# Ternary quantisation of the feed-forward weights: from ScalarE and GpSimd to GpSimd alone, ahead of the rest of its group

## The chip, the cores and the metric

One core of a Trainium2 chip. The time is that of the device for one execution, in microseconds; a kernel's figure is the median of its runs. A profiled execution gives the trace; its span goes from the first to the last instruction of the program.

Engines: TensorE (PE), its weight loads (PEld), VectorE (DVE), ScalarE (ACT), GpSimd (POOL). SyncE (SP) issues nearly all DMAs, in order.

## The reference, cut to what matters

A decoder layer with a layer norm behind each of its three parts: attention with 4-bit quantised projections, a cross attention, and a feed-forward part whose weights are ternary. 4 sequences of 512 tokens, 512 channels, 32 heads of 16. Of the feed-forward part:

```python
def weight_quant(w):
    scale = jnp.clip(jnp.mean(jnp.abs(w)), EPS)
    q = jnp.clip(jnp.round(w / scale), -1.0, 1.0) * scale
    return w + jax.lax.stop_gradient(q - w)

def h_bitlinear(x, w):
    xq = act_quant(fwht(x))          # Hadamard rotation, 8 bits per token
    wq = weight_quant(w)
    return jnp.einsum('bsh,oh->bso', xq, wq)

gate = h_bitlinear(hidden_states, w_gate)      # 512 -> 2048
up = h_bitlinear(hidden_states, w_up)
return h_bitlinear(jax.nn.silu(gate) * up, w_down)
```

So each of the three weight matrices (2048 x 512) becomes -1, 0 or 1 times one scale: -1 below half the scale's negative, 1 above half the scale.

## The kernel before, in words

Three stages follow each other. The first (up to about 150 us) quantises the inputs and the projection weights, computes the cross attention's maps, and reads all feed-forward weights once for their mean magnitudes; at its end f_rec holds, for each matrix, one over the scale. The second is the attention loop (to about 689 us). The third does the output projection, the cross attention's product, and the feed-forward part.

**The attention loop** goes over 32 groups (`groups`): 4 sequences (b) by 8 groups (r) of 4 heads. n is the group's number, and each engine has its own function for a group: `pe_period`, `act_period`, `dve_period`, `pool_period`, `sp_period`. Each engine runs its own list in the order in which it is written, and they meet at semaphores alone. A group has 8 steps (u). In each step TensorE computes two score tiles for the group after (L978; VectorE takes their row maxima, L1134) and two transposed ones for this group (L996, into the two banks of st_bank; ScalarE takes their exponentials, L1083). Each of the two banks is written again only after its exponential. In four steps TensorE also multiplies probabilities with values (L1010).

At the start of a group VectorE splits the 16 maxima into three bfloat16 parts (nm, L1153 to L1162), TensorE turns them (L983), VectorE copies them out (nm_T, L1177), and SP stores them (L1267).

**Even groups** also make the queries and keys of a later pair of groups (`pe_qk`, `dve_y`): for each of the two, ScalarE takes the high part (`act_high`, L1090, at u=4 and 6), GpSimd the residual (L1219), ScalarE the middle part (`act_middle`, L1094, at u=5 and 7), GpSimd the low part (L1221); SP then writes them out in six stores (L1248). Residuals and low parts are `pool_parts`. **Odd groups** project the values of the next sequence (`pe_v`) and normalise a context tile on GpSimd (`pool_norm`, L695) once SP's spread of reciprocals (L683, L685) has landed. In groups with r=7 GpSimd also centres four tiles (L791), in those with r=1 it scales four (L797), from the second or third sequence on.

**The order on SP** in a group (`sp_period`): store nm_T; load the stacks for the group after next (L1258); in odd groups the spread; the store of an attention result (`sp_pv`, L1263); in odd groups the read of the sums (`sp_sums`, L668), behind a wait for the landing of the `sp_pv` stores; in even groups the six stores of the parts, behind waits for the low parts, and the reciprocals (L672); and last the load of a piece of feed-forward weights (`sp_ffn`, L1291).

**The feed-forward weights** pass through the loop in 24 pieces of 128 x 1024 (PIECES), one in each of the groups 0 to 23. A piece is loaded in the group before into one half of f_ring (two halves, which lie in woT), and only after the piece before last in the same half is done (f_done). In its group ScalarE, at u=3, multiplies by f_rec and adds the constant MAGIC, which rounds (`act_ffn`, L1295); GpSimd clips to MAGIC -1 and +1 (L1301) and takes MAGIC away into f_int_all (L1303). In GpSimd's list this stands behind the residuals (even) or the normalisation (odd).

Of the kernel before, what the change touches and what calls it, by code (L numbers as in the profile page):

```python
# [18 lines left out]
P = 128  # L19
# [28 lines left out]
def decoder_layer(nc, io):  # L48
    whole = ExitStack()
    with whole:  # L50
# [806 lines left out]
        with stage:  # L857
# [9 lines left out]
            rs_bc = sb("rs_bc", [P, S])  # L867
            woT = sb("woT", [P, KD, D])
            f_ring = woT[:].rearrange("p k d -> p (k d)").rearrange("p (i c) -> p i c", i=2)
            bo_row = sb("bo_row", [NC, D])  # L870
            bo_tmp = w_int["v"][0:NC].rearrange("p k c m -> p (k c m)").bitcast(F32).rearrange("p (i d) -> p i d", i=2)
            bo_bf = bias_parts["v"][0:NC].rearrange("p k m -> p (k m)")
            neg_max = sb("neg_max", [P, 2, 16])
# [235 lines left out]
            def act_period(act, g):  # L1109
                even = g.h == 0  # L1110
                for u in range(8):
                    g_T, w = steps_T(g, u)
                    if g_T:
                        act_exp(act, g_T, w)
                    if u == 0 and not g.second:
                        act_pv(act, g + -2)
                    if even and g.has(2):
                        if u in HIGH_AT:
                            act_high(act, g.tile(2), HIGH_AT.index(u))
                        if u in MIDDLE_AT:  # L1120
                            act_middle(act, g.tile(2), MIDDLE_AT.index(u))
                    if g.b > 1 and g.r == 3 and 1 <= u <= 4:
                        act_round(act, g.b - 2, u - 1)
                    if u == 3 and g.n < PIECES:
                        act_ffn(act, g.n)
                    if not even and u == V_AT + 1 and g.b < NB - 1:

                        if g.b and g.s == 0:
                            act.wait_ge(pv_mm, 2 * 2 * KD * g.b)
                        act_v(act, g.b + 1, g.s)  # L1130
# [51 lines left out]
            def dve_context(dve, g, u):  # L1182
# [21 lines left out]
                if g.b == NB - 1:  # L1204
                    if g.r == 1 and u == 4:
                        dve_rtb_row(dve, 0, misc)
                    if g.r == 3 and u == 7:
                        dve.wait_ge(v_mm, KD * NB)
                        dve_bias_o(dve, 0, 0, misc, bo_row[:], bo_tmp, bo_bf)
                    if g.r == 4 and 1 <= u < 6:  # L1210
                        dve_bias_o(dve, 0, u, misc, bo_row[:], bo_tmp, bo_bf)

            def pool_parts(pool, t):

# [7 lines left out]
                                       ALU.subtract).then_inc(low_ready, 1)  # L1222

            def pool_period(pool, g):
                if g.h == 0 and g.has(2):
                    pool_parts(pool, g.tile(2))
                if g.h == 1 and g.n >= 5:
                    pool_norm(pool, (g.n - 5) // 2, rs_bc[:])
                if g.n < PIECES:
                    pool_ffn(pool, g.n)  # L1230
                if g.b and g.r == 7:
                    for ct in range(KD):
                        pool_center(pool, g.b - 1, ct)
# [31 lines left out]
            def sp_period(sp, g):  # L1265
# [14 lines left out]
                if g.n + 1 < PIECES:  # L1280
                    sp_ffn(sp, g.n + 1)
                if g.n == PIECES:
                    need(sp, "f_done", 2 * PIECES)
                    load_wo(sp, woT[:], bo_row[:])
                if (g.b, g.r) == (NB - 1, 5):
                    sp.wait_ge(qk_mm, 2 * NM)
                    sp.dma_start(x1[:], x_rows[0]).then_inc(E("x_in"), 16)

            def sp_ffn(sp, c):
                need(sp, "f_done", 2 * (c - 1))  # L1290
                sp.dma_start(f_ring[:, c % 2, :], io["ffn"][c]).then_inc(f_in[c % 2], 16)  # L1291

            def act_ffn(act, c):
                act.wait_ge(f_in[c % 2], 16 * (PIECES // FBUF + c // 2 + 1))
                did(act.activation(f_ring[:, c % 2, :], f_ring[:, c % 2, :], ACT.Identity, bias=magic[:],  # L1295
                                   scale=f_rec[:, c // FPW:c // FPW + 1]), "f_round")

            def pool_ffn(pool, c):
                raw = f_ring[:, c % 2, :]
                need(pool, "f_round", c + 1)  # L1300
                did(pool.tensor_scalar(raw, raw, MAGIC - 1.0, MAGIC + 1.0, ALU.max, ALU.min), "f_done")  # L1301
                need(pool, "f_done", 2 * c + 1)
                did(pool.tensor_scalar(f_int_all[:, c, :], raw, -MAGIC, None, ALU.add), "f_done")  # L1303

            def groups(eng, period):

# [942 lines left out]
```

## Time and profile before

| | us |
|---|---|
| three runs | 1225.28 (median), 1222.91, 1225.84 |
| profiled execution, its time | 1230.77 |
| its span | 1229.0 |
| PE, DVE, ACT, POOL busy | 969.5, 860.4, 694.1, 373.8 |
| mean granted TensorE clock | 0.918 of full speed |

A row of the timeline gives start and duration in us, the engine, the line of the kernel, the operation, what it writes and reads, and in brackets the time for which the engine had stood idle before it and who released it. SPq rows are the issues of DMAs, not their transfers. A row of the windows gives the stretch, its length, and for PE, PEld, DVE, ACT and POOL the busy time with the number of instructions, then the granted TensorE clock (1.00 is 2.4 GHz), the DMA engines' busy share and GB/s. A row of a source line gives shortest, median and longest duration in ns, and first and last start in us. Spans on POOL are rough.

### The profile page before, as it was taken

Reading aid. Unit: us, or ns where it says so; the run is one execution under the profiler, and the core shown is the slowest. Engines: PE = TensorE matmul, PEld = TensorE weight load, DVE = VectorE, ACT = ScalarE, POOL = GpSimd, SP = SyncE. Lnnn points to the kernel's source line nnn. Section 1 sums busy time; section 2 is a strip of 40 time slices with the busy share of each in tenths; the row PEclk is TensorE's granted clock in tenths of the full one; section 3 lists DMA queues with packets and bytes.
Section 4 is the critical chain, followed back from the end, with each engine's and each line's share of the span. In section 5 each row is a group of like instructions: output and inputs, shape, how many; then the busy total and the mean of one; then the engine's idle time right before and its main releaser. Section 6 shows DMA issues by size and latency. Waiting matters only on the chain. (4 is left out here: it accounts for less than half of the span.)

```text
span 1229.0 us, 13431 instructions
## 1 busy us (share of the span) xinstructions
PE 969.5 (79%) x4128; PEld 366.9 (30%) x4128; DVE 860.4 (70%) x1624; ACT 694.1 (56%) x1106; POOL 373.8 (30%) x296
## 2 busy tenths in 40 slices
PE   1556478988999888988988578988897799779565
PEld 0222112222222222222222243334443444334222
DVE  6854468888888998999896548837764776475245
ACT  2775425777777767776767224436633663365255
POOL 1000135546566567565301243122003101310000
PEclk9878668999999998999999879989998999899877
DMA  9873154555555555555523321321052105102500
GB/s 333 279 281 132 46 165 138 156 168 179 169 179 174 173 156 173 162 173 157 156 64 109 117 77 26 68 44 69 3 129 42 69 18 125 29 1 51 119 1 35
DMA packets 90798, 145.80 MB, mean 119 GB/s; under 512 B 12356, under 2 KB 52164, under 8 KB 89095
## 3 DMA queue, kind: packets, MB, share of 16 engines
q1 hardware_dynamic: 87270, 132.36, 36.6%
q10 hardware_dynamic: 3456, 12.58, 2.9%
q8 instruction: 33, 0.54, 0.2%
q14 instruction: 39, 0.31, 0.1%
HBM read 85.54 MB, written 42.21 MB: 104 GB/s over the span
## 5 line engine op out<-in xcount | busy, mean ns | idle before, releaser
L1134 DVE TENSOR_REDUCE neg_max<-banks 128x1 f32<-128x512 f32 x512 | 332.1, 683 | 55.1 <-PE banks L978 52.4
L1083 ACT ACTIVATE probs<-banks 128x512 f32<-128x512 f32 x512 | 278.9, 598 | 120.4 <-PE banks L996 115.8
L996 PE MATMUL banks<-q_st,k_st 99*128 99x512 bf16 x512 | 196.8, 387 | 34.1 <-ACT probs L1083 27.7
L978 PE MATMUL banks<-k_st,q_st 96*128 96x512 bf16 x512 | 201.6, 398 | 4.3 <-DMA k_st<-qk_parts 2.3
L1010 PE MATMUL banks<-probs,v_st 128*32 128x512 f32 x1024 | 138.2, 612 | 8.9 <-ACT pv_z L1107 7.7
L1670 PE MATMUL banks<-q_T,f_int_all 128*128 128x512 bf16 x512 | 125.8, 387 | 19.5 <-DVE h_ring L1691 19.4
L1464 POOL TENSOR_TENSOR rstd<-vare,half 128x1 f32<-128x1 f32 x48 | 26.8, 558 | 358.2 <-DVE vare L1456 358.2
L1729 PE MATMUL banks<-hz,I_h 128*128 128x512 f32 x128 | 71.3, 698 | 35.3 <-DMA hz<-h_turned 32.9
L996 PEld LDWEIGHTS banks<-q_st,k_st 99*128 99x128 bf16 x512 | 49.8, 98 | 133.5 <-ACT probs L1083 72.5
L978 PEld LDWEIGHTS banks<-k_st,q_st 96*128 96x128 bf16 x512 | 50.9, 100 | 127.5 <-DVE neg_max L1134 64.8
L1301 POOL TENSOR_SCALAR woT<-woT 128x1024 f32<-128x1024 f32 x24 | 87.2, 3632 | 2.4 <-ACT woT L1295 0.4
L1680 DVE TENSOR_TENSOR h_ring<-banks,gate_row 128x512 f32<-128x512 f32 x64 | 44.1, 689 | 59.9 <-PE banks L1670 58.3
L1685 ACT ACTIVATE h_ring<-h_ring 128x512 f32<-128x512 f32 x64 | 40.3, 630 | 77.4 <-DVE h_ring L1680 77.4
L1670 PEld LDWEIGHTS banks<-q_T,f_int_all 128*128 128x128 bf16 x512 | 48.7, 99 | 100.6 <-DVE h_ring L1691 28.8
L1708 ACT COPY h_turned<-banks 128x512 f32<-128x512 f32 x64 | 37.1, 582 | 62.0 <-DMA hz<-h_turned 37.2
L1812 PE MATMUL banks<-f_int_all,ctx_q 128*128 128x512 bf16 x256 | 61.5, 388 | 9.1 <-ACT ctx_q L1796 9.1
L1448 PE MATMUL banks<-attn_T,x_T 128*128 128x512 f32 x128 | 60.8, 620 | 9.5 <-DVE x L1487 7.9
L1748 DVE TENSOR_TENSOR h_max<-h_abs,h_max 128x512 f32<-128x512 f32 x60 | 44.4, 741 | 34.1 <-ACT h_abs L1737 32.7
L1734 ACT COPY hz<-banks 128x1024 f32<-128x1024 f32 x32 | 32.4, 1013 | 62.6 <-PE banks L1729 62.6
L1303 POOL TENSOR_SCALAR f_int_all<-woT 128x1024 bf16<-128x1024 f32 x24 | 66.7, 2779 | 2.0
L1702 PE MATMUL banks<-h_ring,had 128*128 128x512 f32 x128 | 64.4, 596 | 2.3 <-ACT h_turned L1708 2.3
L695 POOL TENSOR_TENSOR ctx_q<-ctx_q,rs_bc 128x512 f32<-128x512 f32 x14 | 17.8, 1270 | 153.2 <-DMA ctx_q<-pv_rows 153.2
(260 smaller groups left out, 1506.7 us busy)
## 6 DMA issues: line engine op xcount, KB each, us to landing
hz<-h_turned SPq DMA_DIRECT2D x64, 256.0 KB
f_int_all<-in_ffn_dram ACTq DMA_DIRECT2D x24, 512.0 KB, 6.9
woT<-in_ffn_dram SPq DMA_DIRECT2D x24, 512.0 KB, 3.7
qk_parts<-parts SPq DMA_DIRECT2D x32, 384.0 KB, 2.5
q_st<-qk_parts SPq DMA_DIRECT2D x32, 384.0 KB, 3.9
k_st<-qk_parts SPq DMA_DIRECT2D x32, 384.0 KB, 4.9
qk_parts<-parts SPq DMA_DIRECT2D x32, 256.0 KB, 2.8
pv_rows<-pv_z SPq DMA_DIRECT2D x32, 256.0 KB, 5.1
```

The costliest lines, as they stand in the source:

```text
L978: pe.matmul(s_bank[tile % SB], q_st[g.i][0:KR, j, qt * P:(qt + 1) * P], k_st[g.i][0:KR, j, :], start=True, stop=True).then_inc(s_mm, 1)
L996: pe.matmul(st_bank[i], k_st[g.i][:, j, kt * P:(kt + 1) * P], q_st[g.i][:, j, :], start=True, stop=True).then_inc(st_mm, 1)
L1010: last = pe.matmul(pv_bank[32 * j:32 * j + 32, :], v_st[g.v][:, kt].rearrange("p h d -> p (h d)")[:, (HD + 1) * head:(HD + 1) * head + 2 * ...
L1083: act.activation(probs[ktp][:, j, i, :], st_bank[i], ACT.Exp).then_inc(exp_done, 2)
L1134: dve.tensor_reduce(neg_max[:, g.h, tile:tile + 1], s_bank[tile % SB], AX.X, ALU.max, negate=True).then_inc(max_done, 1)
L1301: did(pool.tensor_scalar(raw, raw, MAGIC - 1.0, MAGIC + 1.0, ALU.max, ALU.min), "f_done")
L1303: did(pool.tensor_scalar(f_int_all[:, c, :], raw, -MAGIC, None, ALU.add), "f_done")
L1448: last = pe.matmul(bank, x1_T[:, k, t], attn_T[:, k, :], start=k == 0, stop=k == KD - 1)
L1670: last = pe.matmul(bank, f_int[w][:, k * FF + ch.start:k * FF + ch.stop], q1_T[:, k, :], start=k == 0, stop=k == KD - 1)
L1702: did(pe.matmul(H_BANK[i % 2], had[:], h[:, g % HRING, :], start=True, stop=True), "h1_mm")
L1729: last = pe.matmul(pair_banks(p)[:, a, :], I8_h16[:], hz[:, 2 * p + a, :], start=True, stop=True)
L1812: last = pe.matmul(down_bank(b, t), q2_T[:, k, token_tile(t)], f_int["down"][:, k * D:(k + 1) * D], start=k == 0, stop=k == FK - 1)
```

## The change

ScalarE's step goes. GpSimd compares the raw weights, times f_rec, with -0.5 (a first tile, 1 where below) and with 0.5 (a second, 1 where above), and subtracts the first from the second into f_int_all. The first tile is bfloat16 and takes the bytes of bo_row, which becomes 128 partitions tall. In `pool_period` the piece stands first, ahead of `pool_parts` and `pool_norm`. f_done now counts three a piece.

```diff
--- before.py
+++ after.py
@@ -867,7 +867,9 @@
             rs_bc = sb("rs_bc", [P, S])
             woT = sb("woT", [P, KD, D])
             f_ring = woT[:].rearrange("p k d -> p (k d)").rearrange("p (i c) -> p i c", i=2)
-            bo_row = sb("bo_row", [NC, D])
+            bo_row = sb("bo_row", [P, D])
+            f_low = bo_row[:].bitcast(BF16)
+            bo_row = bo_row[0:NC]
             bo_tmp = w_int["v"][0:NC].rearrange("p k c m -> p (k c m)").bitcast(F32).rearrange("p (i d) -> p i d", i=2)
             bo_bf = bias_parts["v"][0:NC].rearrange("p k m -> p (k m)")
             neg_max = sb("neg_max", [P, 2, 16])
@@ -1121,8 +1123,6 @@
                             act_middle(act, g.tile(2), MIDDLE_AT.index(u))
                     if g.b > 1 and g.r == 3 and 1 <= u <= 4:
                         act_round(act, g.b - 2, u - 1)
-                    if u == 3 and g.n < PIECES:
-                        act_ffn(act, g.n)
                     if not even and u == V_AT + 1 and g.b < NB - 1:
 
                         if g.b and g.s == 0:
@@ -1206,9 +1206,9 @@
                         dve_rtb_row(dve, 0, misc)
                     if g.r == 3 and u == 7:
                         dve.wait_ge(v_mm, KD * NB)
-                        dve_bias_o(dve, 0, 0, misc, bo_row[:], bo_tmp, bo_bf)
+                        dve_bias_o(dve, 0, 0, misc, bo_row, bo_tmp, bo_bf)
                     if g.r == 4 and 1 <= u < 6:
-                        dve_bias_o(dve, 0, u, misc, bo_row[:], bo_tmp, bo_bf)
+                        dve_bias_o(dve, 0, u, misc, bo_row, bo_tmp, bo_bf)
 
             def pool_parts(pool, t):
 
@@ -1222,12 +1222,12 @@
                                        ALU.subtract).then_inc(low_ready, 1)
 
             def pool_period(pool, g):
+                if g.n < PIECES:
+                    pool_ffn(pool, g.n)
                 if g.h == 0 and g.has(2):
                     pool_parts(pool, g.tile(2))
                 if g.h == 1 and g.n >= 5:
                     pool_norm(pool, (g.n - 5) // 2, rs_bc[:])
-                if g.n < PIECES:
-                    pool_ffn(pool, g.n)
                 if g.b and g.r == 7:
                     for ct in range(KD):
                         pool_center(pool, g.b - 1, ct)
@@ -1280,27 +1280,25 @@
                 if g.n + 1 < PIECES:
                     sp_ffn(sp, g.n + 1)
                 if g.n == PIECES:
-                    need(sp, "f_done", 2 * PIECES)
-                    load_wo(sp, woT[:], bo_row[:])
+                    need(sp, "f_done", 3 * PIECES)
+                    load_wo(sp, woT[:], bo_row)
                 if (g.b, g.r) == (NB - 1, 5):
                     sp.wait_ge(qk_mm, 2 * NM)
                     sp.dma_start(x1[:], x_rows[0]).then_inc(E("x_in"), 16)
 
             def sp_ffn(sp, c):
-                need(sp, "f_done", 2 * (c - 1))
+                need(sp, "f_done", 3 * (c - 1))
                 sp.dma_start(f_ring[:, c % 2, :], io["ffn"][c]).then_inc(f_in[c % 2], 16)
 
-            def act_ffn(act, c):
-                act.wait_ge(f_in[c % 2], 16 * (PIECES // FBUF + c // 2 + 1))
-                did(act.activation(f_ring[:, c % 2, :], f_ring[:, c % 2, :], ACT.Identity, bias=magic[:],
-                                   scale=f_rec[:, c // FPW:c // FPW + 1]), "f_round")
-
             def pool_ffn(pool, c):
-                raw = f_ring[:, c % 2, :]
-                need(pool, "f_round", c + 1)
-                did(pool.tensor_scalar(raw, raw, MAGIC - 1.0, MAGIC + 1.0, ALU.max, ALU.min), "f_done")
-                need(pool, "f_done", 2 * c + 1)
-                did(pool.tensor_scalar(f_int_all[:, c, :], raw, -MAGIC, None, ALU.add), "f_done")
+                raw, w = f_ring[:, c % 2, :], c // FPW
+                need(pool, "f_done", 3 * c)
+                pool.wait_ge(f_in[c % 2], 16 * (PIECES // FBUF + c // 2 + 1))
+                did(pool.tensor_scalar(f_low, raw, f_rec[:, w:w + 1], -0.5, ALU.mult, ALU.is_lt), "f_done")
+                need(pool, "f_done", 3 * c + 1)
+                did(pool.tensor_scalar(raw, raw, f_rec[:, w:w + 1], 0.5, ALU.mult, ALU.is_gt), "f_done")
+                need(pool, "f_done", 3 * c + 2)
+                did(pool.tensor_tensor(f_int_all[:, c, :], raw, f_low, ALU.subtract), "f_done")
 
             def groups(eng, period):
```

## Rows read from the trace of the kernel before

**Rows 1.** The page, part 1: busy time, share of the span, instructions.
```profile
PE 969.5 (79%) x4128; PEld 366.9 (30%) x4128; DVE 860.4 (70%) x1624; ACT 694.1 (56%) x1106; POOL 373.8 (30%) x296
```

**Rows 2.** Windows of groups 12 and 26: length, busy time by engine, clock, DMA.
```profile
363.50:378.30 14.80, 14.05 (x79) 4.29 (x75) 12.70 (x25) 11.60 (x22) 11.03 (x6) 1.00 0.43 121
...
587.80:601.70 13.90, 13.30 (x74) 3.98 (x71) 12.60 (x25) 10.57 (x20) 8.67 (x8) 1.00 0.34 103
```

**Rows 3.** Timeline, 373 to 404 us: start, duration, engine, line, operation, [idle before].
```profile
373.82 1.16 POOL L1219 TENSOR_TENSOR rest<-y,parts 128x512 f32<-128x512 f32 x1 [2.30 <-ACT parts L1090]
...
379.15 1.16 POOL L1221 TENSOR_TENSOR parts<-rest,parts 128x512 bf16<-128x512 f32 x1 [0.73 <-ACT parts L1094]
...
382.39 0.46 SPq L1291 DMA_DIRECT2D woT<-in_ffn_dram  x1
...
386.01 1.24 ACT L1295 ACTIVATE woT<-woT,magic,f_rec 128x1024 f32<-128x1024 f32 x1
...
387.77 0.45 SPq L1263 DMA_DIRECT2D pv_rows<-pv_z  x1
...
387.88 0.38 PE L996 MATMUL banks<-q_st,k_st 99*128 99x512 bf16 x1 [1.11 <-ACT probs L1083]
...
393.40 1.26 POOL L695 TENSOR_TENSOR ctx_q<-ctx_q,rs_bc 128x512 f32<-128x512 f32 x1 [6.51 <-DMA ctx_q<-pv_rows]
...
394.02 0.59 SPq L668 DMA_DIRECT2D c_sums<-pv_rows  x1
...
394.66 0.46 SPq L1291 DMA_DIRECT2D woT<-in_ffn_dram  x1
...
403.68 1.16 POOL L1219 TENSOR_TENSOR rest<-y,parts 128x512 f32<-128x512 f32 x1 [2.44 <-ACT parts L1090]
```

**Rows 4.** Source line L1291, the loads of weight pieces in the loop.
```profile
DMA to landing us min/median/max: 3.5/3.7/4.8
```

**Rows 5.** Groups of GpSimd by shape: busy us, mean ns of one | idle before.
```profile
L1301 POOL TENSOR_SCALAR woT<-woT 128x1024 f32<-128x1024 f32 x24 | 87.2, 3632 | 2.4 <-ACT woT L1295 0.4
L1303 POOL TENSOR_SCALAR f_int_all<-woT 128x1024 bf16<-128x1024 f32 x24 | 66.7, 2779 | 2.0
...
L1221 POOL TENSOR_TENSOR parts<-rest,parts 128x512 bf16<-128x512 f32 x32 | 37.1, 1158 | 27.7 <-ACT parts L1094 27.7
...
L791 POOL TENSOR_TENSOR ctx_q<-ctx_q,c_bias 128x512 f32<-128x512 f32 x16 | 16.7, 1074 | 0.0
...
L255 POOL TENSOR_TENSOR xT<-xT,x_bias 128x2048 f32<-128x2048 f32 x2 | 7.2, 3618 | 24.5 <-DVE x_cmax L193 24.5
```

**Rows 6.** Source line L1159, ns min/median/max.
```profile
L1159 DVE CAST nm<-nm_f x32: 157/494/1209, 184.4 to 663.0; 128x16 bf16<-128x16 f32 x32
```

**Rows 7.** Timeline of TensorE at two long stops.
```profile
296.64 0.38 PE L996 MATMUL banks<-q_st,k_st 99*128 99x512 bf16 x1 [1.87 <-ACT probs L1083]
...
486.07 0.59 PE L996 MATMUL banks<-q_st,k_st 99*128 99x512 bf16 x1 [2.77 <-ACT probs L1083]
```

**Rows 8.** Windows, columns as in rows 2: the clock behind those stops.
```profile
297.30:300.70 3.40, 3.40 (x10) 1.13 (x8) 1.83 (x3) 1.06 (x3) 0.00 (x0) 0.50 0.63 224
...
485.10:491.90 6.80, 5.83 (x16) 1.83 (x20) 3.61 (x6) 4.06 (x8) 1.71 (x2) 0.50 0.47 152
```

**Rows 9.** Timeline of GpSimd and SP: first residuals of pairs, one load.
```profile
191.51 1.16 POOL L1219 TENSOR_TENSOR rest<-y,parts 128x512 f32<-128x512 f32 x1 [14.80 <-ACT parts L1090]
...
221.45 1.16 POOL L1219 TENSOR_TENSOR rest<-y,parts 128x512 f32<-128x512 f32 x1 [9.82 <-ACT parts L1090]
...
436.30 1.31 POOL L1219 TENSOR_TENSOR rest<-y,parts 128x512 f32<-128x512 f32 x1
...
461.31 0.46 SPq L1291 DMA_DIRECT2D woT<-in_ffn_dram  x1
...
470.83 1.17 POOL L1219 TENSOR_TENSOR rest<-y,parts 128x512 f32<-128x512 f32 x1
...
534.83 1.16 POOL L1219 TENSOR_TENSOR rest<-y,parts 128x512 f32<-128x512 f32 x1 [2.41 <-ACT parts L1090]
```

## Prediction

> **What bounds the kernel now.** I read the page's busy shares first: TensorE is busy 79% of the span, VectorE 70%, ScalarE 56%, GpSimd 30% [rows 1]. The change touches only the attention loop, so the windows of single groups come next. In an even group (12, by its window) TensorE is busy 14.05 of 14.80 us, VectorE 12.70, ScalarE 11.60 [rows 2]. So the loop runs at TensorE's pace, and TensorE takes turns with ScalarE over two banks: whatever stops ScalarE stops it within a microsecond. The timeline of groups 12 to 14 shows both things that matter here [rows 3]. First, ScalarE's quantising activation (L1295, 1.24 us at 386.01) is followed by a TensorE matmul that had idled 1.11 us for an exponential: the activation is on the path. Second, the rhythm of a pair of groups is 29.86 us, from one first residual (L1219 at 373.82) to the next (403.68). I write T for that start and count from it.
>
> SP's queue decides when a piece of feed-forward weights is in SBUF. SP works in order. In an even group it waits for the residuals, issues six stores and only then the next load, at T+8.6 (382.39). In an odd group it waits for the landing of the store it issued at 387.77 before it issues the read of the sums (394.02), and the load follows at 394.66, T+20.8 [rows 3]. A load lands 3.5 to 4.8 us after its issue, median 3.7 [rows 4]. So the odd piece is in SBUF at T+12.3 and the even one at T+24.5. Today that is early enough: ScalarE asks at u=3, and GpSimd comes to it a whole step later.
>
> **The change, part by part.** *Removed:* 24 activations of 1.24 us on ScalarE, and 24 times two GpSimd instructions of 3.63 and 2.78 us [rows 5]. The relief on TensorE's path is about 1.0 us a group: 1.11 idle in an odd one [rows 3], and an even group without the activation (26) lasts 13.90 us where group 12 lasts 14.80 [rows 2]. The loop would then need some 27.9 us a pair.
>
> *Added:* three GpSimd instructions a piece. No comparison stands in the trace. The nearest row is the two-step tensor_scalar of the same size, 3.63 us; the one-step form takes 2.78, so a step is worth 0.85 [rows 5]. From below I bound a comparison by the subtraction of the same size, from above by two more steps, 5.3 us. The subtraction is between 1.16 us (512 elements) and 3.62 (2048) [rows 5]: in a straight line 1.98 at 1024. I take 3.63 for each comparison, since multiply-and-compare is a two-step tensor_scalar like maximum-and-minimum. The bfloat16 output and the scalar taken from a tile no row shows in this form; I cost them at nothing, inside the same bounds. A piece: 3.63 + 3.63 + 1.98 + three gaps of 0.09 = 9.5 us, against 6.5 before.
>
> *Moved:* GpSimd's order was residuals, piece, normalisation, piece. It becomes piece, residuals, piece, normalisation: the same alternation, each piece one place earlier. GpSimd now arrives at the odd piece when the residuals end, T+6.5 (379.15 and 1.16), but the load lands at T+12.3: it stands 5.8 us. Then 9.5 for the piece (T+21.8) and 1.35 for the normalisation, whose data is there at T+19.6 [rows 3]: T+23.1. The even piece has landed at T+24.5. It is 9.5 long, and **the next residuals are queued behind it**. They were wanted at T+29.86, and with the relief at about T+27.9. ScalarE's middle parts wait for the residual, the exponentials wait behind them in ScalarE's queue, TensorE and VectorE wait for the exponentials. As SP's two loads hang on T itself (its stores follow the residuals, its odd group opens with a wait for that group's nm_T copy), the delay is not caught up: each pair lasts T+24.5 plus 9.5, 34.0. The relief of ScalarE lies in that stall and is worth nothing.
>
> Two corrections. VectorE's small casts are now and then held while GpSimd works (L1159: 0.16 us at least, 0.49 in the median, 1.21 at most) [rows 6]; in the odd group GpSimd now stands idle when they run, so I take 0.4 off. And TensorE would stand some 5 us in each pair. The trace shows what follows such a stop: after 1.87 us of idle time (296.64) the granted clock was 0.50 for 3.4 us, after 2.77 us (486.07) it was 0.50 from 485.1 to 491.9; behind 1.11 us a matmul still took 0.38 us where it took 0.59 at 486.07 [rows 3, 7, 8]. 0.50 is 1.2 GHz of 2.4. In 3.4 us at half speed 1.7 us of work is lost, and these microseconds lie just behind T, ahead of the nm_T copy that SP's odd group hangs on. So a pair is 24.5 - 0.4 + 1.7 + 9.5 = **35.3 us**.
>
> The sum over the loop, each pair against its own row [rows 3, 9]:
> - 191.51 to 221.45 (29.94 us; no normalisation and no store to wait for): 12.3 + 9.5 + 9.5 = 31.3, so +1.4.
> - 221.45 to 403.68, six pairs, 182.2 us: 6 x 35.3 = 211.8, so +29.6.
> - 403.68 to 436.30 (32.6): GpSimd also centres four tiles, 4 x 1.07 [rows 5], ahead of the even piece now: 12.3 + 9.5 + 1.35 + 4.3 + 9.5 = 37.0, so +4.4.
> - 436.30 to 470.83 (34.5): the load is issued at 461.31, T+25.0; 25.0 + 3.7 - 0.4 + 1.7 + 9.5 = 39.5, so +5.0.
> - 470.83 to 534.83, two pairs, 64.0: 70.6, so +6.6.
> - After 534.83 no piece stands ahead of the residuals: two relieved groups (-2.0) behind one more stop (+1.7): 0.
> - Before 191.51 ScalarE has one activation less: -1.2.
>
> Sum +45.8. The profiled execution took 1230.8 us (span 1229.0), so it would be 1276.6; that execution lies 5.5 above the median of the three runs, 1225.3, from which the forecast is **1271**. Everything else costs nothing: the larger bo_row is space alone; f_done counts to three a piece, reached with GpSimd's own last instruction; SP's wait for it ahead of a load is for the piece before last, done by T. The feed-forward stage after the loop is as it was.
>
> **Rivals.**
> 1. *A comparison costs a step more* (4.48 us). A piece is 11.2. The loads still decide (12.3 + 11.2 + 1.35 = 24.9, under 25.8), nine pairs grow by 1.7, the first and the centring one by 3.4: +22, **1293**. For it: the step in rows 5. Against: maximum and minimum are comparisons too, and cost what they cost.
> 2. *The clock doesn't fall*, because TensorE works ahead in the stop and its idle time is shorter than 1.9 us: ten times 1.7 less, **1254**. Against: with two banks it can work ahead by little more than a microsecond.
> 3. *The other side: the pieces are in time.* GpSimd's own work in a pair is 6.5 + 9.5 + 1.35 + 9.5 = 26.9 us, under the 27.9 of the relieved loop. If its loads landed when it arrives, nothing would stop ScalarE and 24 groups would win 1.0 each: **1201**. It decides from the point at which the even piece is done by T+27.9, so if it can start by T+18.4, or be done in under 4 us. For it: SP could be ahead if its waits resolved sooner. Against: both loads stand behind waits that hang on T.
> 4. *The comparisons are as quick as a subtraction* (1.98 each, a piece 6.2): T+24.5 - 0.4 + 6.2 = 30.3 against 29.9, no long stop, **1228**. Against: the same instruction form takes 3.63 today.
>
> **How the numbers follow.** My forecast 0.47, rival 1 0.24, rival 2 0.17, rival 3 0.07, rival 4 0.05. The likeliest's 1271 is the prediction. The range 1240 to 1302 takes in rivals 1 and 2 with their scatter and leaves out the faster side and comparisons of 5.3 us. 0.3% is 3.7 us, about what can be told from nothing: faster 0.08 (rival 3 and a little of 4), same 0.04, slower 0.88.
>
> **What would show it.** In the profile after: comparisons near 3.63 us each and a subtraction near 2.0; ahead of the odd piece GpSimd idle some 5 us for the DMA of woT, and 1 to 3 ahead of the even one; the odd and even loads still at T+8.6 and about T+21 to 22; ScalarE's L1094 waiting 4 to 6 us in each pair for the residual; pairs of about 35 us; the granted clock at half for some microseconds after each. It is wrong if GpSimd doesn't stand for the loads, if residuals start on time, or if ScalarE's stop doesn't reach TensorE.

## The result and the profile after

The changed kernel takes 1266.9 us (median of 4 runs, 1265.59 to 1271.24), the kernel before beside it 1225.56 (1222.91 to 1227.65): a ratio of 1.0345, 95% interval 1.0311 to 1.0378. It is slower by 3.4%; 1271 was forecast. The spans of the two profiled executions differ by 40.4 us (1269.4 and 1229.0).

The page, part 1, and of part 4 the shares of the chain that ended last by engine and the line under it:

```profile
PE 977.0 (77%) x4077; PEld 368.3 (29%) x4128; DVE 869.0 (68%) x1624; ACT 669.0 (53%) x1082; POOL 448.0 (35%) x320
...
PE 29%; POOL 18%; DVE 14%; DMA 11%; issue 9%; ACT 5%; SPq 2%; POOLq 0%; ACTq 0%; DVEq 0%
PE banks L1668 6%; POOL bo_row L1297 5%; POOL woT L1299 5%; DVE neg_max L1134 4%; DMA woT<-in_ffn_dram 4%; DMA hz<-h_turned 3%; PE banks L1810 3%; PE banks L1700 3%; PE banks L1012 3%; DMA pv_rows<-pv_z 3%; PE banks L1446 3%; POOL f_int_all L1301 2%; PE banks L1727 2%; PE banks L998 2%; POOL rest L1219 2%
```

Beside [rows 1] ScalarE is busy 25 us less and GpSimd 74 more. That alone would say nothing about the time. The chain shows more: the two comparisons, the transfer of the piece (woT) and the attention result's store (pv_rows) stand on it. It can't be laid beside the kernel before's, which the profile follows back only to 686 us and not into the loop; the comparison of the two rests on the timelines.

The three GpSimd instructions, one group each (busy us, mean ns | idle before them), and two rows of waits (in total, times, longest; then ScalarE's wait ahead of the middle parts: total, times), against [rows 5]:

```profile
L1299 POOL TENSOR_SCALAR woT<-woT,f_rec 128x1024 f32<-128x1024 f32 x24 | 89.4, 3727 | 2.2
L1297 POOL TENSOR_SCALAR bo_row<-woT,f_rec 128x1024 bf16<-128x1024 f32 x24 | 89.0, 3707 | 84.2 <-DMA woT<-in_ffn_dram 84.0
L1301 POOL TENSOR_TENSOR f_int_all<-woT,bo_row 128x1024 bf16<-128x1024 f32 x24 | 51.0, 2125 | 2.0
```

```profile
POOL bo_row L1297 <- DMA woT<-in_ffn_dram: 84.0, 18, 7.1
```

```profile
  POOL rest L1219: 56.4, 24
```

A comparison costs 3.71 and 3.73 us, the subtraction 2.13; with the two gaps a piece is 9.7, and the next residual starts 9.8 us behind the landing of the load. GpSimd, which never waited for a load before, stands 84 us for them, and ScalarE 56 us for GpSimd's residual.

The timeline of one ordinary pair (groups 8 and 9, T = 324.29), rows of GpSimd, SP, ScalarE and TensorE, to be laid beside [rows 3]:

```profile
324.29 1.15 POOL L1219 TENSOR_TENSOR rest<-y,parts 128x512 f32<-128x512 f32 x1
...
329.61 1.15 POOL L1221 TENSOR_TENSOR parts<-rest,parts 128x512 bf16<-128x512 f32 x1 [0.73 <-ACT parts L1096]
...
332.85 0.45 SPq L1291 DMA_DIRECT2D woT<-in_ffn_dram  x1
...
336.63 3.71 POOL L1297 TENSOR_SCALAR bo_row<-woT,f_rec 128x1024 bf16<-128x1024 f32 x1 [5.87 <-DMA woT<-in_ffn_dram]
...
345.26 0.59 SPq L668 DMA_DIRECT2D c_sums<-pv_rows  x1
345.90 0.46 SPq L1291 DMA_DIRECT2D woT<-in_ffn_dram  x1
...
346.31 1.27 POOL L695 TENSOR_TENSOR ctx_q<-ctx_q,rs_bc 128x512 f32<-128x512 f32 x1
...
349.65 3.71 POOL L1297 TENSOR_SCALAR bo_row<-woT,f_rec 128x1024 bf16<-128x1024 f32 x1 [2.06 <-DMA woT<-in_ffn_dram]
...
357.24 2.12 POOL L1301 TENSOR_TENSOR f_int_all<-woT,bo_row 128x1024 bf16<-128x1024 f32 x1
359.32 1.15 POOL L1219 TENSOR_TENSOR rest<-y,parts 128x512 f32<-128x512 f32 x1
...
360.50 0.62 ACT L1096 CAST parts<-rest 128x512 bf16<-128x512 f32 x1 [4.79 <-POOL rest L1219]
...
361.67 0.61 PE L998 MATMUL banks<-q_st,k_st 99*128 99x512 bf16 x1 [3.71 <-ACT probs L1085]
```

Read it from the top. The parts end at T+6.5 and GpSimd idles 5.87 us, since the load was issued at T+8.6. The odd piece runs from T+12.3 to T+22.0, the normalisation follows without a gap, and GpSimd idles again, 2.06 us, for the load issued at T+21.6. The even piece starts at T+25.4 and the next residual at T+35.0. ScalarE had waited 4.79 us for it, TensorE 3.71 us for ScalarE.

Windows of that pair and of the low clock behind its end (columns as in [rows 2]):

```profile
324.30:359.30 35.00, 28.93 (x143) 8.01 (x145) 26.60 (x47) 20.94 (x39) 24.86 (x12) 0.95 0.53 152
...
360.80:367.60 6.80, 5.93 (x18) 1.31 (x19) 3.02 (x7) 4.80 (x10) 3.46 (x3) 0.50 0.49 172
```

The first residuals of the pairs that were forecast, against [rows 3, 9]:

```profile
191.42 1.16 POOL L1219 TENSOR_TENSOR rest<-y,parts 128x512 f32<-128x512 f32 x1 [6.27 <-ACT parts L1092]
...
222.78 1.15 POOL L1219 TENSOR_TENSOR rest<-y,parts 128x512 f32<-128x512 f32 x1
...
429.58 1.15 POOL L1219 TENSOR_TENSOR rest<-y,parts 128x512 f32<-128x512 f32 x1
...
466.48 1.15 POOL L1219 TENSOR_TENSOR rest<-y,parts 128x512 f32<-128x512 f32 x1
503.45 1.15 POOL L1219 TENSOR_TENSOR rest<-y,parts 128x512 f32<-128x512 f32 x1
...
574.10 1.15 POOL L1219 TENSOR_TENSOR rest<-y,parts 128x512 f32<-128x512 f32 x1
```

| stretch of the loop | before | forecast | after |
|---|---|---|---|
| first pair | 29.9 | 31.3 | 31.4 |
| six pairs | 182.2 | 211.8 | 206.8 |
| the pair with centring | 32.6 | 37.0 | 36.9 |
| the next | 34.5 | 39.5 | 37.0 |
| two pairs | 64.0 | 70.6 | 70.7 |

The sum of the differences is 39.4 of the 40.4 us: nearly all of it lies between the first residuals of groups 0 and 22.

Not every pair is bound like the one shown. In the pairs from 191.4, 222.8, 254.4, 429.6 and 466.5 us GpSimd never waits for the even piece; it works without a gap from the odd piece's landing to the next residual. The one with scaling, from 466.48 (its even load landed at 492.4, ahead of the last of four scaling instructions):

```profile
489.76 4.05 POOL L797 TENSOR_TENSOR ctx_q<-ctx_q,c_cmax 128x512 f32<-128x512 f32 x4
493.78 3.71 POOL L1297 TENSOR_SCALAR bo_row<-woT,f_rec 128x1024 bf16<-128x1024 f32 x1
```

The even load decides in the other six that hold two pieces.

### The profile page after: what moved, and what is told of

Read it like the earlier page. It is cut to its first block, busy times and chain, and to the rows that moved or that the text cites. A ratio compares the mean times of both kernels' runs of the same rounds, so it can differ in the third digit from the quotient of the medians.

```text
span 1269.4 us, 13403 instructions
## 1 busy us (share of the span) xinstructions
PE 977.0 (77%) x4077; PEld 368.3 (29%) x4128; DVE 869.0 (68%) x1624; ACT 669.0 (53%) x1082; POOL 448.0 (35%) x320
## 3 DMA queue, kind: packets, MB, share of 16 engines
q1 hardware_dynamic: 87270, 132.36, 35.4%
## 4 chain that ended last, share of the span: by engine, by line
PE 29%; POOL 18%; DVE 14%; DMA 11%; issue 9%; ACT 5%; SPq 2%; POOLq 0%; ACTq 0%; DVEq 0%
PE banks L1668 6%; POOL bo_row L1297 5%; POOL woT L1299 5%; DVE neg_max L1134 4%; DMA woT<-in_ffn_dram 4%; DMA hz<-h_turned 3%; PE banks L1810 3%; PE banks L1700 3%; PE banks L1012 3%; DMA pv_rows<-pv_z 3%; PE banks L1446 3%; POOL f_int_all L1301 2%; PE banks L1727 2%; PE banks L998 2%; POOL rest L1219 2%
## 5 line engine op out<-in xcount | busy, mean ns | idle before, releaser
L998 PE MATMUL banks<-q_st,k_st 99*128 99x512 bf16 x512 | 202.7, 399 | 53.1 <-ACT probs L1085 46.8
L980 PE MATMUL banks<-k_st,q_st 96*128 96x512 bf16 x512 | 205.4, 406 | 2.7 <-DMA k_st<-qk_parts 2.1
L1012 PE MATMUL banks<-probs,v_st 128*32 128x512 f32 x1024 | 145.4, 641 | 8.7 <-ACT pv_z L1109 7.5
L1668 PE MATMUL banks<-q_T,f_int_all 128*128 128x512 bf16 x498 | 122.4, 384 | 21.5 <-DVE h_ring L1689 19.7
L1297 POOL TENSOR_SCALAR bo_row<-woT,f_rec 128x1024 bf16<-128x1024 f32 x24 | 89.0, 3707 | 84.2 <-DMA woT<-in_ffn_dram 84.0
L1727 PE MATMUL banks<-hz,I_h 128*128 128x512 f32 x128 | 69.9, 685 | 35.3 <-DMA hz<-h_turned 32.6
L1299 POOL TENSOR_SCALAR woT<-woT,f_rec 128x1024 f32<-128x1024 f32 x24 | 89.4, 3727 | 2.2
L1668 PEld LDWEIGHTS banks<-q_T,f_int_all 128*128 128x128 bf16 x512 | 48.7, 99 | 100.3 <-DVE h_ring L1689 28.8
L1706 ACT COPY h_turned<-banks 128x512 f32<-128x512 f32 x64 | 37.2, 582 | 61.2 <-DMA hz<-h_turned 34.6
L1746 DVE TENSOR_TENSOR h_max<-h_abs,h_max 128x512 f32<-128x512 f32 x60 | 44.8, 746 | 32.9 <-ACT h_abs L1735 31.6
L345 PE MATMUL banks<-f_int_all 128*128 128x512 f32 x32 | 22.1, 855 | 47.6 <-DMA had<-in_had_dram 26.4
```

What stands on the lines that cost most here:

```text
L980: pe.matmul(s_bank[tile % SB], q_st[g.i][0:KR, j, qt * P:(qt + 1) * P], k_st[g.i][0:KR, j, :], start=True, stop=True).then_inc(s_mm, 1)
L998: pe.matmul(st_bank[i], k_st[g.i][:, j, kt * P:(kt + 1) * P], q_st[g.i][:, j, :], start=True, stop=True).then_inc(st_mm, 1)
L1012: last = pe.matmul(pv_bank[32 * j:32 * j + 32, :], v_st[g.v][:, kt].rearrange("p h d -> p (h d)")[:, (HD + 1) * head:(HD + 1) * head + 2 * ...
L1297: did(pool.tensor_scalar(f_low, raw, f_rec[:, w:w + 1], -0.5, ALU.mult, ALU.is_lt), "f_done")
L1299: did(pool.tensor_scalar(raw, raw, f_rec[:, w:w + 1], 0.5, ALU.mult, ALU.is_gt), "f_done")
L1668: last = pe.matmul(bank, f_int[w][:, k * FF + ch.start:k * FF + ch.stop], q1_T[:, k, :], start=k == 0, stop=k == KD - 1)
```

## Experiments

T is again the start of a pair's first residual. Each ratio is to the kernel before, run on the same chip; its median lay at 1229.0, 1230.4 and 1226.6 us in the three sets. "Ordinary pairs" are those from group 4 on without centring or scaling and without what follows from them on ScalarE (the pair from group 18).

| kernel | median us | ratio, 95% interval |
|---|---|---|
| no_piece | 1202.3 | 0.979 (0.974 to 0.984) |
| early_loads | 1244.1 | 1.012 (1.006 to 1.017) |
| old_place | 1236.4 | 1.005 (1.003 to 1.007) |
| packed | 1218.8 | 0.992 (0.988 to 0.995) |
| act_left_out | 1213.8 | 0.989 (0.985 to 0.992) |
| one_step | 1243.1 | 1.012 (1.008 to 1.016) |
| packed_moved | 1218.2 | 0.992 (0.989 to 0.995) |
| one_step_packed | 1218.9 | 0.992 (0.989 to 0.995) |
| one_step_front | 1213.6 | 0.991 (0.989 to 0.994) |
| one_step_old | 1223.9 | 0.998 (0.995 to 1.000) |

**no_piece.**
```diff
-                did(pool.tensor_scalar(f_low, raw, f_rec[:, w:w + 1], -0.5, ALU.mult, ALU.is_lt), "f_done")
...
+                for i in range(3):
+                    did(pool.memset(f_int_all[:, c, (0, 512, 768)[i]:(512, 768, 1024)[i]], 1.0), "f_done")
```

> The changed kernel with the three GpSimd instructions of a piece left out (three short memsets fill the piece's tile in their place, so the feed-forward weights are not the reference's). Loads, waits and order stay. Late loads and a long piece together (my theory): the loads are as late as ever (T+8.6 and T+21), but a piece of about 1.5 us that starts at T+24.5 is done before the residuals are wanted, so nothing stops ScalarE, its 24 activations are gone, a pair takes about 28 us, and the time is 1203 us (1198 to 1210). If the late loads or the place at the front cost by themselves, it stays above 1240. If ScalarE's activation was never on the path, it is 1225.

Measured 1202.3. The window of one ordinary pair:

```profile
306.40:334.90 28.50, 27.25 (x147) 7.91 (x145) 25.26 (x48) 20.92 (x40) 7.95 (x11) 1.00 0.62 188
```

A pair takes 28.5 us, with TensorE busy 27.25 of them at full clock, though the loads come as late as in the changed kernel. So a late load and a place at the front cost nothing by themselves: the piece's length behind the load does. It also sets the floor. 28.5 is what the loop needs without any quantising work. That is 1.4 less than the 29.9 of [rows 3], the base of my forecast, and 1.9 less than the mean of the six ordinary pairs before (30.4, as two of them took 30.5 and 32.3).

**early_loads.**
```diff
                     sp_stack(sp, g + 2)
+                if g.n + 1 < PIECES:
+                    sp_ffn(sp, g.n + 1)
                 if g.h == 1 and g.n >= 5:
                     sp_spread(sp, (g.n - 5) // 2, rs_bc[:])
...
-                if g.n + 1 < PIECES:
-                    sp_ffn(sp, g.n + 1)
```

> The changed kernel with SP issuing each load of a piece ahead of the group's waits (behind the stacks, ahead of the spread, the sums and the parts' stores). Late loads (my theory): GpSimd finds each piece in SBUF. Residuals end at T+6.5, the odd piece at T+16.4; the normalisation's data comes at T+19.6, so the even piece runs from T+20.9 to T+30.8: that is the pair, 30.8 us against 35 in the changed kernel, some 1228 us (1222 to 1238, the upper end if TensorE's clock still falls). Rival, the three instructions' length alone sets the time, whatever the loads do: 1255 to 1267.

Measured 1244.1: 1.2% over the kernel before, where the changed kernel lies 3.4% over it, and above my range. GpSimd's timeline of the pair from 282.34:

```profile
282.34 1.15 POOL L1219 TENSOR_TENSOR rest<-y,parts 128x512 f32<-128x512 f32 x1
...
288.80 3.70 POOL L1297 TENSOR_SCALAR bo_row<-woT,f_rec 128x1024 bf16<-128x1024 f32 x1
...
302.72 1.28 POOL L695 TENSOR_TENSOR ctx_q<-ctx_q,rs_bc 128x512 f32<-128x512 f32 x1 [4.21 <-DMA ctx_q<-pv_rows]
303.98 3.71 POOL L1297 TENSOR_SCALAR bo_row<-woT,f_rec 128x1024 bf16<-128x1024 f32 x1
...
313.66 1.15 POOL L1219 TENSOR_TENSOR rest<-y,parts 128x512 f32<-128x512 f32 x1
```

The wait for the weights is gone (5.3 us in all), and another has come up in its place: the even piece stands behind the normalisation, whose data comes at T+20.4. That was 19.6 in [rows 3]. The load is now issued ahead of the spread, but old_place, where it is not, has 19.3 to 20.4 there, so that cause isn't shown. The moved loads also land later, 5.8 us behind their issue in the median for 3.7:

```profile
DMA to landing us min/median/max: 4.0/5.8/7.7
```

The pair is 31.3 us, and 32.6 to 33.6 in the three whose start had a stop of TensorE and a stretch at half the clock. So some two thirds of the loss went with the lateness. Rival 3 of the prediction (pieces in time, 1201 us) falls: it had left out the normalisation's own data.

**old_place.**
```diff
             def pool_period(pool, g):
-                if g.n < PIECES:
-                    pool_ffn(pool, g.n)
                 if g.h == 0 and g.has(2):
                     pool_parts(pool, g.tile(2))
                 if g.h == 1 and g.n >= 5:
                     pool_norm(pool, (g.n - 5) // 2, rs_bc[:])
+                if g.n < PIECES:
+                    pool_ffn(pool, g.n)
```

> The changed kernel with the piece back behind the residuals and the normalisation; three instructions and late loads as in the changed kernel. Late loads (my theory): here they are not late, since GpSimd comes to each piece one place later. Residuals to T+6.5, the even piece to T+16.4, normalisation from T+19.6, the odd piece from T+20.9 to T+30.8: a pair of 30.8 us, some 1230 us (1222 to 1240). Rival, the length of the three instructions alone: 1255 to 1267, as with the piece in front.

Measured 1236.4, inside the range: of the changed kernel's 3.4% the place alone gives back all but 0.5. The loads are issued as late as ever, and GpSimd waits for none of them. Its ordinary pairs take 29.9 to 31.3 us (29.8 to 32.3 before).

**packed.**
```diff
+                if g.h == 0 and g.n < PIECES:
+                    pool_ffn(pool, g.n, range(1, 3) if g.n else range(3))
                 if g.h == 0 and g.has(2):
                     pool_parts(pool, g.tile(2))
+                if g.h == 1 and g.n < PIECES:
+                    pool_ffn(pool, g.n)
+                    if g.n + 1 < PIECES:
+                        pool_ffn(pool, g.n + 1, range(1))
                 if g.h == 1 and g.n >= 5:
                     pool_norm(pool, (g.n - 5) // 2, rs_bc[:])
```
(the third argument of `pool_ffn` says which of the three instructions it issues; loads as in early_loads.)

> Loads early as in early_loads, and GpSimd does the even piece's first comparison in the odd group ahead of the normalisation, so that it works while the normalisation's data is on its way. My theory: residuals to T+6.5, odd piece to T+16.4, first comparison to T+20.1, normalisation to T+21.4, the rest of the even piece to T+27.4, just under the 27.9 us that the loop needs without ScalarE's activation. Pairs of 28.0 to 28.5 us, 1204 us (1198 to 1212). Rival, the port that VectorE and GpSimd share: with GpSimd busy nearly always VectorE's small casts are held, and the relief is eaten: 1215 to 1230.

Measured 1218.8: quicker than the kernel before, but 15 us above my theory's 1204 and inside the range that I gave the rival. Ordinary pairs take 28.4 to 29.6, and a wait for the weights is left in each of them: the even piece's load, issued at about T+12, lands at T+17.5 to T+18.7, GpSimd idles 1.5 to 2.7 us for it, and then works without a gap into the next residual, which in each starts 10.9 to 11.0 us behind the landing. One of them, from 309.69:

```profile
327.40 3.71 POOL L1303 TENSOR_SCALAR bo_row<-woT,f_rec 128x1024 bf16<-128x1024 f32 x1 [1.53 <-DMA woT<-in_ffn_dram]
...
338.20 1.16 POOL L1219 TENSOR_TENSOR rest<-y,parts 128x512 f32<-128x512 f32 x1
```

So the shared port, my rival, isn't shown to be what is missing here. The pair with centring takes 35.4:

```profile
420.31 1.28 POOL L695 TENSOR_TENSOR ctx_q<-ctx_q,rs_bc 128x512 f32<-128x512 f32 x1
421.54 4.04 POOL L791 TENSOR_TENSOR ctx_q<-ctx_q,c_bias 128x512 f32<-128x512 f32 x4
425.56 3.71 POOL L1305 TENSOR_SCALAR woT<-woT,f_rec 128x1024 f32<-128x1024 f32 x1
429.35 2.13 POOL L1307 TENSOR_TENSOR f_int_all<-woT,bo_row 128x1024 bf16<-128x1024 f32 x1
431.43 1.15 POOL L1219 TENSOR_TENSOR rest<-y,parts 128x512 f32<-128x512 f32 x1
```

GpSimd works without a gap from 416.6, when the weights land, to 431.4: the landing and GpSimd's own work behind it, 14.8 us with the centring, are the bound.

**act_left_out.**
```diff
-                    if u == 3 and g.n < PIECES:
-                        act_ffn(act, g.n)
...
-                need(pool, "f_round", c + 1)
+                pool.wait_ge(f_in[c % 2], 16 * (PIECES // FBUF + c // 2 + 1))
```
(to the kernel before.)

> The kernel before with ScalarE's 24 activations left out and GpSimd's two instructions kept in their old place (the weights are clipped raw, so they are not the reference's). It measures what ScalarE's activation costs by itself. My theory: it alone sets the difference between 29.9 us a pair and the 28.5 that the loop took without the GpSimd instructions; GpSimd is done at T+27.5, in time. 1204 us. Rival, VectorE held at the shared port makes up part of it: then GpSimd's presence keeps it at 1212 or more.

Measured 1213.8, the rival's side. By the ratios ScalarE's activation by itself is worth 1.1%, some 14 us; leaving out GpSimd's work as well brings 2.1% (no_piece), and the other 12 us go with GpSimd's two instructions. GpSimd isn't late here: in each ordinary pair it idles 1.2 to 1.8 us ahead of the first residual. The 12 us show in an ordinary pair (29.4 us against 28.5, VectorE busy 26.51 against 25.26):

```profile
307.60:337.00 29.40, 27.26 (x145) 7.96 (x146) 26.51 (x49) 20.93 (x40) 18.71 (x9) 1.00 0.62 184
```

and in VectorE's small subtraction (ns, shortest, median, longest), here and in no_piece:

```profile
L1154 DVE TENSOR_TENSOR nm_f<-neg_max,nm x32: 155/683/1210, 184.5 to 653.0; 128x16 f32<-128x16 f32 x32
```

```profile
L1156 DVE TENSOR_TENSOR nm_f<-neg_max,nm x32: 157/170/1208, 184.8 to 635.9; 128x16 f32<-128x16 f32 x32
```

**one_step.**
```diff
-                    dve.reciprocal(f_rec[:], ws_col[:])
+                    for i, part in enumerate((-0.5, 0.5)):
+                        dve.tensor_scalar(f_half[:, i], ws_col[:], part, None, ALU.mult)
...
-                did(pool.tensor_scalar(f_low, raw, f_rec[:, w:w + 1], -0.5, ALU.mult, ALU.is_lt), "f_done")
+                did(pool.tensor_scalar(f_low, raw, f_half[:, 0, w:w + 1], None, ALU.is_lt), "f_done")
...
-                did(pool.tensor_scalar(raw, raw, f_rec[:, w:w + 1], 0.5, ALU.mult, ALU.is_gt), "f_done")
+                did(pool.tensor_scalar(raw, raw, f_half[:, 1, w:w + 1], None, ALU.is_gt), "f_done")
```

> The changed kernel with each comparison in one step: the raw weight against half the scale, from a tile that VectorE fills once, in place of the product with one over the scale. Order and loads as in the changed kernel. My theory: a comparison is 2.8 us in place of 3.7, a piece 8.0 in place of 9.8. The even load still lands at T+25, so a pair shrinks by one piece's saving, from 35 to 33 us, and the time is 1243 us (1236 to 1250). If the piece's length didn't matter and the lateness alone did, it stays at 1262 or more; if only the length mattered, both pieces' savings count, 3.7 a pair, 1227.

Measured 1243.1, the number expected. The comparisons:

```profile
L1300 POOL TENSOR_SCALAR woT<-woT,f_half 128x1024 f32<-128x1024 f32 x24 | 68.3, 2846 | 2.2
L1298 POOL TENSOR_SCALAR bo_row<-woT,f_half 128x1024 bf16<-128x1024 f32 x24 | 68.3, 2846 | 95.4 <-DMA woT<-in_ffn_dram 95.2
```

A piece is 1.75 us shorter, and an ordinary pair lies between 32.2 and 34.5 where it was 34.2 to 35.7. The odd piece's saving turns into waiting for the even load (95 us of idle time in all, 84 in the changed kernel): of two pieces in an ordinary pair only the one behind the late load counts. The saving of 2.2% is what the chain asked for.

**packed_moved** (to packed):
```diff
-                if g.b and g.r == 7:
+                if (g.b == 2 and g.r == 0) or (g.b == 3 and g.r in (0, 7)):
                     for ct in range(KD):
-                        pool_center(pool, g.b - 1, ct)
-                if g.b > 1 and g.r == 1:
+                        pool_center(pool, g.b - (1 if g.r == 7 else 2), ct)
+                if (g.b, g.r) in ((2, 2), (3, 1)):
```

> packed, with the four centring and the four scaling instructions of GpSimd one group later, behind the residuals. In packed the pairs from 396 and 431 us took 35.4 and 35.0 us where the kernel without GpSimd's pieces took 30.1 and 31.1: centring stood ahead of the even piece's rest. My theory: the first falls to 30.5, the second to 32, the third stays at 31.7, and the time is 1210 us (1206 to 1214). If those pairs are long for another reason, 1218 as packed.

Measured 1218.2, no gain. The centring pair fell from 35.4 to 32.0, the next stayed at 34.9, and the one at 553 grew to 34.7 (30.8 in packed). VectorE, GpSimd and TensorE from 434 us:

```profile
434.03 4.04 POOL L791 TENSOR_TENSOR ctx_q<-ctx_q,c_bias 128x512 f32<-128x512 f32 x4
434.23 0.86 DVE L1153 CAST nm<-neg_max 128x16 bf16<-128x16 f32 x1
...
437.15 0.95 DVE L1159 CAST nm<-nm_f 128x16 bf16<-128x16 f32 x1
...
439.33 0.22 PE L985 MATMUL banks<-identb,nm 128*128 128x128 bf16 x1 [3.73 <-DVE nm L1162]
```

In no_piece, at the same place, the two casts take 0.17 us each and TensorE waits a third as long:

```profile
432.04 0.22 PE L985 MATMUL banks<-identb,nm 128*128 128x128 bf16 x1 [1.21 <-DVE nm L1162]
```

VectorE's small instructions are held while GpSimd's centring runs. TensorE waits for them, 3.7 us instead of 1.2, and its clock was at 0.50 for the 3.4 us that followed.

**one_step_packed** (packed_moved with the comparisons of one_step):
```diff
-                        ins = pool.tensor_scalar(f_low, raw, rec, -0.5, ALU.mult, ALU.is_lt)
+                        ins = pool.tensor_scalar(f_low, raw, f_half[:, 0, w:w + 1], None, ALU.is_lt)
...
-                        ins = pool.tensor_scalar(raw, raw, rec, 0.5, ALU.mult, ALU.is_gt)
+                        ins = pool.tensor_scalar(raw, raw, f_half[:, 1, w:w + 1], None, ALU.is_gt)
```

> packed_moved with the one-step comparisons: GpSimd needs some 24 us in an ordinary pair and never holds up the residuals. My theory: as quick as the kernel without the pieces, 1204 us (1201 to 1208), 2% under the kernel before. Rival, the shared port: GpSimd's instructions hold VectorE's small ones and 1210 or more is left.

Measured 1218.9, a miss, for the same reason: ordinary pairs are at 28.7 to 29.1, but the stop of 3.73 us is there, from 433.2 in this run, and one of 3.32 from 560.2; the pairs with them take 35.4 and 35.7.

**one_step_front** (one_step_packed with centring and scaling as in packed):
```diff
-                if (g.b == 2 and g.r == 0) or (g.b == 3 and g.r in (0, 7)):
+                if g.b and g.r == 7:
...
-                if (g.b, g.r) in ((2, 2), (3, 1)):
+                if g.b > 1 and g.r == 1:
```

> packed (centring and scaling in their old place) with the one-step comparisons. In packed_moved the centring ran beside VectorE's levels and held them: a stop of 3.7 us on TensorE at T+8.8. My theory: back in the old place that stop is gone, and with pieces of 8 us GpSimd is done at T+31.3 in the centring pair (the loop needs 30.1) and at T+31.8 in the next (31.1). 1209 us (1205 to 1213). Rival, the port's cost in ordinary pairs sets the rest: 1216 to 1220 as the last two.

Measured 1213.6: 0.88% under the kernel before and the best of those that do all of the layer's work. Its ordinary pairs take 28.7 to 29.0 and the pair at 553 is back at 30.6. The pairs with centring (32.7) and scaling (34.6) are still longer than in no_piece (30.1, 31.1): 6 of the 12 us between the spans of the two profiles. An ordinary pair is 0.1 to 0.5 longer; where the remainder lies is open. Against packed, packed_moved and one_step_packed the intervals overlap; the spacing of the pairs tells them apart, the ratios don't.

**one_step_old** (old_place with the comparisons of one_step):
```diff
-                did(pool.tensor_scalar(f_low, raw, f_rec[:, w:w + 1], -0.5, ALU.mult, ALU.is_lt), "f_done")
+                did(pool.tensor_scalar(f_low, raw, f_half[:, 0, w:w + 1], None, ALU.is_lt), "f_done")
```

> The changed kernel with the one-step comparisons and the piece back behind the residuals and the normalisation; loads as in the kernel before. So it is the kernel before with three GpSimd instructions, 8.0 us, in place of ScalarE's activation and two, 6.5 us. My theory: residuals to T+6.5, even piece to T+14.5, normalisation from T+19.6 to T+20.9, odd piece to T+28.9: ordinary pairs of 29.2 us against 29.9, the centring pair 33 to 34, and 1217 us (1212 to 1222). If the place or SP's late loads hurt here too, 1228 or more.

Measured 1223.9, a ratio that just includes no change: above my range by 2 us. Ordinary pairs are at 29.0 to 29.4 as expected; the pairs with centring or scaling and the one behind (33.9 to 35.6) took what they had won.

## Why the prediction was right

Step by step, as the prediction put them:

- *The loads come too late for GpSimd's new place.* Right for the odd piece in every pair and for the even one in six pairs. GpSimd idled 5.87 and 2.06 us for them in the pair shown (5.8 and 1.4 forecast), and no_piece, early_loads and one_step bear the chain out from three sides.
- *The even piece stands ahead of the residuals and holds ScalarE, then TensorE.* Right: 4.79 and 3.71 us of waits in the pair shown, and all but 0.5% gone with the piece back in its place (old_place).
- *A comparison costs what maximum-and-minimum costs.* Right: 3.71 and 3.73 against 3.63. Rival 1, a step more for the comparison, falls. The subtraction was 2.13 for an interpolated 1.98, so a load's landing was followed by 9.8 us and not by 9.5. The Trainium skill, "GPSIMD Engine Reference", § 7 Performance pitfalls for Q7 kernels, gives compare-and-select bodies 2.03 cycles an element where 1.03 is reached by unrolling; a surcharge of that size doesn't show between 3.63 and 3.73 us. The Trainium skill's "1-input is roughly line-rate" (the same page, § 4.1 Engine selection) doesn't agree with a one-input comparison of 3.7 us for 1024 elements.
- *The clock falls behind each stop.* Right in kind: behind 3.71 us it was at 0.50 for 6.8 us. The term of 1.7 us a pair was too large. In the ordinary pairs that the even load decides, it landed at T+24.7 where no stretch was at 0.50 (from 539.6), at T+24.9 and T+25.2 with 3.4 us of it, at T+25.7 and T+25.9 with 6.8: 0.7 more in the mean of four, measured against a single pair. The 0.4 that I took off for VectorE's casts isn't seen either: 24.5 less 0.4 was forecast without the clock, 24.7 came. Rival 2 lies nearer than I gave it credit for, but the clock did fall.
- *35.3 us for each of six pairs.* This term was mis-sized: 206.8 for 211.8. The first of them took 31.6 us, since before group 5 SP has no spread ahead of its load and the pair is bound by GpSimd's two pieces, as I had worked out for the very first pair alone. The second took 34.2 and was bound by GpSimd's list too; its odd load landed late, at T+13.4. That the other four took 35.25 in the mean is in part luck: the even load landed 0.4 us earlier than in my sum, and the piece was 0.3 longer.
- *39.5 us for the pair with scaling.* It took 37.0, and here the step itself was wrong: I let the even load decide. It was issued at T+22.4 and not T+25.0 (my row was of a pair in which TensorE had stood for VectorE) and landed at T+26.0, but GpSimd came to it only at T+27.3. I had left out the four scaling instructions ahead of the even piece, 4.0 us, though I had counted the four of centring in the pair before. From the odd landing on GpSimd's own list is the bound in both, and they took 36.9 and 37.0.
- *The relief of ScalarE is 2.0 us a pair and worth nothing in the stall.* The second half is right. The first was put down to ScalarE alone: all quantising work together was worth 1.9 a pair in the mean (1.4 from the 29.9 that I started from), of which ScalarE's activation is 1.2 (act_left_out, ordinary pairs of 28.8 to 29.5), 14 us over the loop where 24 were put. It entered the sum only ahead of the first pair and behind group 22.

The six pairs and the one with scaling make -5.0 and -2.5 of the difference; +1.1 came ahead of the first pair, where the activation less saved next to nothing, and +1.2 behind group 22. So 45.8 was forecast and 40.4 seen in the spans.

## What to carry to other kernels

Before an instruction moves to the front of an in-order queue, work out when its input lands in the new place: the queue that loads it was arranged for the old one. A stall of an engine at 35% busy became the bound because one short instruction (1.15 us), for which everybody waits, stood behind one long piece that waited for a transfer. Look for the rhythm (here the pair) and add up the chain between two of its beats, for each kind of pair its own: the engine's whole list in it counts (here the scaling); a saving outside that chain (here the odd piece of an ordinary pair, here ScalarE's 1.24 us) is worth nothing until the chain is shorter than the loop.

## What the runs showed of the hardware

- GpSimd: a two-step tensor_scalar of 128x1024 takes 3.63 to 3.73 us whether its steps are maximum and minimum, or a product and a comparison, with scalars as numbers or from a tile, with float32 or bfloat16 output. With one step it takes 2.78 to 2.85. A subtraction of two tiles takes 2.13.
- VectorE's small casts and subtractions (128x16) between 190 and 650 us of the twelve profiles: none of the 426 that overlapped no GpSimd instruction took over 0.18 us. Of 485 beside a GpSimd tensor_tensor 356 took over 0.4, and of 501 beside a tensor_scalar 205. In the kernel before, each of the 22 that started in the first 0.7 us of a tensor_scalar ended 1.06 or 1.07 us after that one's start; the 18 that started 1.2 to 2.1 us into it took 0.16 to 0.18. So a tensor_scalar held them at its start, and not throughout.
- TensorE's clock between 190 and 650 us of the twelve profiles: each of the 21 idle stretches of 3.3 us or more had a stretch at 0.50 (1.2 GHz) with it, beginning up to 2.2 us before the engine took up work again or up to 1.7 us after; of the 34 between 1.7 and 3.0 us 22 had one. It lasted 3.4 or 6.8 us. Two more stretches at 0.50 came behind shorter stops, of 1.6 us (one_step_packed) and 1.04 us (one_step_front).
- A load of a weight piece took 3.7 us to land in the median at the end of a group's list on SP, and 5.8 to 6.0 where it was issued right behind the loads of the stacks (early_loads and the four packed kernels). Why isn't shown.
